# Mixing the tokens of the last units on VectorE instead of TensorE, with their scaling moved there and new call orders

## The reference

```python
# block 1: a long convolution per channel (K decays geometrically), a projection, layer norms
y = layer_norm(xn + gelu(conv(xn, K) + D_vec * xn) @ W_proj.T + b_proj, gamma, beta)
t = x + layernorm(y)
# block 2: tn = layernorm(t), tn_prev = tn of the token before (0 for the first of a sequence)
xr = mu_r * tn + (1.0 - mu_r) * tn_prev
xk = mu_k * tn + (1.0 - mu_k) * tn_prev
r = sigmoid(xr @ W_r.T)
k_act = square(relu(xk @ W_k.T))
out = t + layernorm(r * (k_act @ W_v.T))
```

## Time and profile before

| what | value |
|---|---|
| median of three runs | 150.51 us (150.22 to 150.79) |
| the profiled execution | 150.25 us, span 148.5 us, mean granted TensorE clock 0.988 |
| TensorE, busy | 135.5 us (91%) |
| VectorE, busy | 130.8 us (88%) |
| ScalarE, busy | 129.6 us (87%) |
| GpSimd, busy | 127.5 us (86%) |
| bytes moved | 8.99 MB |

### The profile page before, as it was taken

The page is one execution under the profiler, slowest core; times in us unless marked ns, Lnnn a source line. Parts: engine busy times, 40 slices in busy tenths (PEclk is TensorE's granted clock), DMA queues, the critical chain, the costliest instruction groups (busy, mean ns, idle before and its releaser), DMA issues.

```text
span 148.5 us, 3239 instructions
## 1 busy us (share of the span) xinstructions
PE 135.5 (91%) x950; PEld 116.0 (78%) x950; DVE 130.8 (88%) x372; ACT 129.6 (87%) x388; POOL 127.5 (86%) x176
## 2 busy tenths in 40 slices
PE   6778888989999999999999999999999999999910
PEld 6667787876988799797979797988887887777900
DVE  0989999999999988999997999998999899339981
ACT  4878999799699999979779999959998988999940
POOL 4599999998989988989896998978999899978282
PEclk9999999999999999999999999999999999999995
DMA  3999900000000002000200002200200200424524
GB/s 89 235 328 272 299 22 0 0 2 0 0 4 0 0 0 77 0 2 0 75 0 0 0 4 71 73 0 7 71 2 0 71 4 0 141 68 138 152 72 141
DMA packets 18705, 8.99 MB, mean 61 GB/s; under 512 B 1536, under 2 KB 18688, under 8 KB 18688
## 3 DMA queue, kind: packets, MB, share of 16 engines
q1 hardware_dynamic: 17840, 8.52, 19.7%
q10 hardware_dynamic: 848, 0.26, 0.7%
HBM read 4.59 MB, written 4.19 MB: 59 GB/s over the span
## 4 chain that ended last, share of the span: by engine, by line
PE 73%; POOL 17%; DVE 4%; DMA 2%; issue 1%; POOLq 1%; ACT 0%
PE ps_k L855 9%; PE ps_k L856 9%; PE ps_r L867 9%; PE ps_r L866 9%; PE ps_tv L876 9%; PE ps_z L833 7%; POOL x_r L227 5%; POOL xn_pow L236 5%; PE ps_tv L846 5%; PE ps_prefix L813 4%; PE ps_z L834 4%; PE ps_xT L805 3%; PE ps_prefix L819 2%; PE ps_prefix L815 2%; DMA a_col<-in_A_param 2%
## 5 line engine op out<-in xcount | busy, mean ns | idle before, releaser
L370 ACT ACTIVATE xn<-x_all,x_bias,x_r 128x128 f32<-128x128 f32 x64 | 26.4, 499 | 1.1 <-POOL x_bias L218 0.6
L867 PE MATMUL ps_r<-mixed_T,tsT 128*128 128x128 f32 x128 | 24.7, 275 | 0.0
L866 PE MATMUL ps_r<-mixed_T,tsT 128*128 128x128 f32 x128 | 24.7, 275 | 0.0
L833 PE MATMUL ps_z<-pv_T,gelu 128*128 128x128 f32 x128 | 22.1, 275 | 0.0
L426 ACT ACTIVATE f_normal<-f,out_bias,yf_r 128x128 f32<-128x128 f32 x48 | 19.8, 493 | 1.5 <-POOL out_bias L285 1.5
L236 POOL TENSOR_TENSOR xn_pow<-xn,pow_token 128x512 f32<-128x512 f32 x16 | 20.3, 1273 | 0.0
L866 PEld LDWEIGHTS ps_r<-mixed_T,tsT 128*128 128x128 f32 x128 | 19.5, 192 | 0.5 <-issue 0.5
L833 PEld LDWEIGHTS ps_z<-pv_T,gelu 128*128 128x128 f32 x128 | 19.4, 191 | 0.5 <-issue 0.5
L389 ACT ACTIVATE junk<-ps_z 128x128 f32<-128x128 f32 x64 | 16.7, 280 | 3.2 <-PE ps_z L834 3.2
L867 PEld LDWEIGHTS ps_r<-mixed_T,tsT 128*128 128x128 f32 x128 | 19.4, 192 | 0.0
L834 PE MATMUL ps_z<-ident,xnT 128*128 128x128 f32 x64 | 17.4, 273 | 0.0
(11 more groups left out here) (112 smaller groups left out, 360.1 us busy)
## 6 DMA issues: line engine op xcount, KB each, us to landing
out_x<-x_all SPq DMA_DIRECT2D x15, 256.0 KB, 2.2
x_all<-in_x SPq DMA_DIRECT2D x7, 512.0 KB, 6.0
x_all<-in_x SPq DMA_DIRECT2D x2, 128.0 KB, 2.8
x_all<-in_x SPq DMA_DIRECT2D x1, 256.0 KB, 3.2
out_x<-x_all SPq DMA_DIRECT2D x1, 128.0 KB, 1.8
out_x<-x_all ACTq DMA_DIRECT2D x1, 128.0 KB, 1.9
w_pv<-in_W_proj ACTq DMA_DIRECT2D x1, 64.0 KB, 2.6
w_pv<-in_W_v ACTq DMA_DIRECT2D x1, 64.0 KB, 4.5
```

The costliest lines, as they stand in the source:

```text
L370: last = a_.activation(tile(xn[u % D], j), xa(u, j), ACT.Identity, bias=col(x_bias, u, j), scale=col(x_r, u, j))
L833: t_.matmul(tile(ps_z[u % 3], j), tile(gelu[u % D], j), pv_T[:, 0, :], start=True, stop=False)
L866: t_.matmul(tile(ps_r, j), tsT[u % D][:, q, l + 1:l + 1 + P], mixed_T[:, 0, :], start=True, stop=False)
L867: last = t_.matmul(tile(ps_r, j), tsT[u % D][:, q, l:l + P], mixed_T[:, 1, :], start=False, stop=True)
```

## The change

For units 13, 14 and 15 the t is now centred and scaled by VectorE (`scale_t_vector`: four instructions per unit, which subtract the mean and multiply by the root), and no longer by GpSimd (13) or ScalarE (14, 15). For these units' gates, and for the keys of 14 and 15, the tokens are mixed before the product: `mix_difference` forms token minus predecessor from `tsT`, `mix_gates` and `mix_keys` multiply it by mu and add the predecessor, each one instruction over 512 columns. `gates` then makes 4 products in place of 8 and `keys` 1 in place of 2, with the plain weights `w_rk_T`. The mixed tokens lie in ring buffers that the first block has left (`xn`, `xn_pow`, `conv_scaled`). The lists of calls of GpSimd, ScalarE, VectorE and TensorE are written anew from beginning to end; SyncE's is as it was.

```diff
-T_ON_POOL = (1, 3, 5, 7, 9, 10, 11, 13)
+T_ON_POOL = (1, 3, 5, 7, 9, 10, 11)
+T_ON_VECTOR = (13, 14, 15)
+MIX_GATES = (13, 14, 15)
+MIX_KEYS = (14, 15)
...
+            def scale_t_vector(u):
+                dve.wait_ge(t_scale, u + 1)
+                after(dve, tT_ready, u - D + 1)
+                for j in range(TILES):
+                    last = v_.scalar_tensor_tensor(tile(t_scaled[u % D], j), xa(u, j), t_raw[:, u * TILES + j, 1:2],
+                                                   col(t_r, u, j).to_broadcast([P, P]), ALU.subtract, ALU.mult)
+                last.then_inc(ts_vector_ready, 1)
...
+            def mix_difference(u):
...
+                dve.wait_ge(tT_copied, u + 1)
+                v_.tensor_tensor(by_halves(xn[u % D]), tsT[u % D][:, :, 1:SEQ + 1], tsT[u % D][:, :, 0:SEQ],
+                                 ALU.subtract).then_inc(mix_differences, 1)
...
+            def mix_gates(u):
+
+                dve.wait_ge(mix_differences, mixed_units.index(u) + 1)
+                v_.scalar_tensor_tensor(by_halves(xn_pow[u % D]), by_halves(xn[u % D]), mu_cols[:, 0:1],
+                                        tsT[u % D][:, :, 0:SEQ], ALU.mult, ALU.add).then_inc(gate_mixed, 1)
+
+            def mix_keys(u):
+
+                dve.wait_ge(mix_differences, mixed_units.index(u) + 1)
+                v_.scalar_tensor_tensor(by_halves(conv_scaled[u % D]), by_halves(xn[u % D]), mu_cols[:, 1:2],
+                                        tsT[u % D][:, :, 0:SEQ], ALU.mult, ALU.add).then_inc(key_mixed, 1)
...
             def keys(u):
...
+                if u in MIX_KEYS:
+                    pe.wait_ge(key_mixed, MIX_KEYS.index(u) + 1)
+                    t_.matmul(ps_k[:], w_rk_T[:, 1, :], conv_scaled[u % D][:], start=True, stop=True).then_inc(k_ready, 1)
+                    return
...
             def gates(u):
...
+                if u in MIX_GATES:
+                    pe.wait_ge(gate_mixed, MIX_GATES.index(u) + 1)
+                    for j in range(TILES):
+                        last = t_.matmul(tile(ps_r, j), tile(xn_pow[u % D], j), w_rk_T[:, 0, :], start=True, stop=True)
+                    last.then_inc(r_ready, 1)
+                    return
```

More of the change, by code:

```diff
@@ L329, in _ @@
[L329 to L349, removed]
+            x_scale_tiles(0, 0, 2); x_scale_tiles(1, 2, 4); x_scale_of(1, 1, 1); xn_times_pow(0); x_scale_of(2, 2, 2)
@@ L840, in transpose_t @@
                     pe.wait_ge(ts_pool_ready, T_ON_POOL.index(u) + 1)
+                elif u in T_ON_VECTOR:
+                    pe.wait_ge(ts_vector_ready, T_ON_VECTOR.index(u) + 1)
                 else:
-                    pe.wait_ge(ts_ready, u + 1 - sum(v < u for v in T_ON_POOL))
+                    pe.wait_ge(ts_ready, u + 1 - sum(v < u for v in T_ON_POOL + T_ON_VECTOR))
                 after(pe, tT_copied, u)
@@ L891, in _ @@
-            prefix_sum(13); keys(6); project(11); values(5); transpose_xn(13); gates(6); transpose_t(7)
-            prefix_sum(14); keys(7); transpose_xn(14); project(12); values(6); gates(7); prefix_sum(15)
-            transpose_t(8); project(13); keys(8); values(7); gates(8); transpose_xn(15); transpose_t(9); project(14)
-            values(8); keys(9); transpose_t(10); gates(9); project(15); values(9); keys(10); transpose_t(11)
+            centre_bias(); keep_busy(3); transpose_xn(0); keep_busy(6); prefix_sum(0); keep_busy(6); transpose_pv()
@@ new lines, in _ @@
+            transpose_xn(1); prefix_sum(1); project(0); transpose_xn(2); prefix_sum(2); project(1); transpose_xn(3)
+            transpose_rk(); prefix_sum(3); project(2); transpose_xn(4); mix_weights(); prefix_sum(4); project(3)
+            prefix_sum(5); transpose_xn(5); project(4); transpose_t(0); prefix_sum(6); transpose_xn(6); gates(0)
+            keys(0); transpose_t(1); prefix_sum(7); keys(1); transpose_xn(7); values(0); project(5); project(6)
+            transpose_xn(8); gates(1); transpose_t(2); prefix_sum(8); values(1); gates(2); keys(2); transpose_t(3)
@@ new lines, in _ @@
+            prefix_sum(9); transpose_xn(9); project(7); values(2); keys(3); prefix_sum(10); gates(3); transpose_xn(10)
+            transpose_t(4); project(8); values(3); keys(4); transpose_xn(11); project(9); prefix_sum(11)
+            transpose_t(5); project(10); gates(4); prefix_sum(12); values(4); transpose_xn(12); gates(5); keys(5)
+            transpose_xn(13); prefix_sum(13); transpose_t(6); project(11); project(12); values(5); keys(6)
+            transpose_t(7); prefix_sum(14); transpose_xn(14); gates(6); keys(7); values(6); gates(7); transpose_xn(15)
@@ L895, in _ @@
+            transpose_t(8); project(13); values(7); keys(8); transpose_t(9); project(14); prefix_sum(15); gates(8)
+            values(8); keys(9); gates(9); transpose_t(10); project(15); values(9); keys(10); transpose_t(11)
             gates(10); values(10); keys(11); transpose_t(12); gates(11); values(11); keys(12); transpose_t(13)
             gates(12); values(12); keys(13); transpose_t(14); gates(13); values(13); keys(14); transpose_t(15)
-            gates(14); keys(15); values(14); gates(15); values(15)
+            gates(14); values(14); keys(15); gates(15); values(15)
```

134 lines of the change are left out of this document (76 added, 58 removed).

## The result

The changed kernel takes 153.48 us (median of five runs, 153.05 to 153.70), the kernel before 150.44 us beside it. The ratio is 1.0193 (95% interval 1.0176 to 1.0211), so it is 1.9% slower. The forecast was 152.2 us, 1.2% slower, with a range that holds the time. The profiled execution took 153.16 us, with a span of 151.4.

What follows compares the result with a forecast made beforehand. VectorE was to become the bound in the last units: 146.84 + 1.3 + 1.03 - 1.7 = 147.5 us for its end, then 3.0 of stores and 1.75 around the span, 152.2 us; range 148.3 to 155.0.

Steps and rivals of the forecast that it cites:

- What bounds: Last units: TensorE paces the end before the change; after it VectorE becomes the bound and limits what TensorE's saving is worth.
- TensorE's cut of 4.4 us: Last units: three gates with half the products save 2.7 us, two keys with one product for two 1.7 us.
- VectorE's added work of 7.9 us: Last units: twelve scaling instructions add 3.1 us and eight mixing instructions over 512 columns 4.8 us.
- Instructions held up, +1.03: VectorE beside GpSimd's additions: one more SBUF-only instruction loses 1.03 us; bounds -1.03 and +6.2.
- The third rival: GpSimd's additions hold up VectorE's new scalings and mixes, four stretches more than now: 155.3 us, chance 0.13.
- New orders ahead of 112.1, -1.7: VectorE before 112.1 us: the new call orders win half of its 3.47 us idle time, -1.7 us.
- ScalarE's and GpSimd's relief, set at nothing: Last units: scalings taken off both engines only bring a tanh or root earlier, for which VectorE won't wait; 0 us.
- Idle time that stays, +1.3: VectorE after 112.1 us: a fifth of its 6.56 us idle time stays, 1.3 us; bounds 0.4 and 3.3.
- The end: VectorE ends at 147.5 us, the last stores take 3.0 us more, and 1.75 us lie around the span.
- The signs: Expected profile: VectorE idle under 2 us after 112, busy 138 to 140; TensorE about 4 us less busy, with late gaps.
- The upper ends: Worst bounds of the terms for idle time, held-up instructions, new orders; all together given as 160 us.
- The first rival: VectorE keeps up: orders win 2.6 us before 112.1, no subtraction is held up, 0.9 us waits stay; 148.9 us, chance 0.30.

Runs made afterwards that it cites:

- the clock kept: Changed kernel plus 28 unread identity transposes on TensorE in its wait before the keys of unit 14: 152.39 us, ratio 1.0129 to the kernel before.
- the end rearranged: Changed kernel without the eight mixing calls, and VectorE's fused addition of unit 13 moved ahead of gate_half(0): 150.02 us, ratio 0.9972 to the kernel before.
- both at once: Changed kernel with GpSimd's additions of units 7 to 9 held back until unit 14's mix, plus 28 TensorE filler transposes: 152.66 us, ratio 1.0138 to the kernel before.

## Why the prediction was right, and by how much it was off

- **What bounds.** Right. TensorE's saving was worth only what VectorE could follow. Without the mixing TensorE paces the end again (the run without it). With all of it the chain that ended last goes through VectorE from 120.7 to 134.6 us and from 143.65 on; between the two it goes through TensorE, which runs at the half clock for the first half of that time.
- **TensorE's cut of 4.4 us.** The products are gone (28 instructions fewer), but I expected a busy time 4 us lower, and it is 0.6 lower, 3.8 short of the 4.4. Some 2.7 us of that went to the half clock: the four groups below take 2.05, 1.06, 1.92 and 1.59 us, against 1.10, 0.63, 1.06 and 1.13 with the clock kept. Of the other 1.1 us, 0.9 lies in the first 20 us (16.60 us against 15.68, for 104 instructions in both kernels), far ahead of the units that the change is about; what makes it I can't say. So the size of the cut was right to some 0.2 us.

```profile
134.58 2.05 PE L899 MATMUL ps_k<-conv_scaled,w_rk_T 128*128 128x512 f32 x2 [3.43 <-DVE conv_scaled L686]
136.42 1.06 PE L888 MATMUL ps_tv<-ident,t_scaled 128*128 128x128 f32 x4
137.27 1.92 PE L913 MATMUL ps_r<-w_rk_T,xn_pow 128*128 128x128 f32 x8
138.98 1.59 PE L928 MATMUL ps_tv<-pv_T,k_act 128*128 128x128 f32 x8
```

- **VectorE's added work of 7.9 us.** Nearly right. Two of the scalings take 1.14 and 1.13 us for four; the difference takes a step of 0.60 us where nothing waits for its result, a mix 0.67.
- **Instructions held up, +1.03.** This is the term that failed. It was +3.3: two of the scaling, one difference, one key mix, while the one subtraction that was long before (1303 ns) is long still (1310; it stands ahead of the gate of unit 12 now, not behind the mixing as the end of unit 13 otherwise does, and beside the addition of unit 5). My reason was that one addition only in the last 20 us had cost anything. But only one had met an instruction that it could hold up; before the change VectorE had hardly any there. The third rival's four stretches came, with 3.3 us in all for its 4.1 (the forecast's 1.03 and 3.1 more), and the run with the additions held back shows the cause.
- **New orders ahead of 112.1, -1.7.** They gave -2.56: VectorE worked 91.16 us from 20 to 112.1 where it worked 88.60. In the run with the new orders and the old scaling VectorE came as far ahead (91.19 us), and it was worth nothing there.
- **ScalarE's and GpSimd's relief, set at nothing.** Right for the changed kernel, where VectorE doesn't wait for a tanh any more. Without mixing no run sets it apart: from 1.0044 with their scaling to 0.9990 without are 0.8 us, but the orders behind the gate of unit 10 differ between these two as well.
- **Idle time that stays, +1.3.** 1.88 us (36.60 less 34.72). More than half is the wait of 1.0 us for the copy of unit 15, which comes late at the half clock; with the clock kept it is gone.
- **The end.** VectorE ends at 148.64 us, forecast 147.5; the span ends 2.8 us later, forecast 3.0; the execution is 1.76 us longer than the span, forecast 1.75.
- **The signs.** VectorE's little idle time after 112 us (1.9) and its share of the chain (12%) came as expected. Its busy time of 141.3 us is above the 138 to 140. The gaps of TensorE that are put down to VectorE stand in front of the keys and the transpose of unit 14 (3.4 and 0.7 us); those in front of the keys and the transpose of unit 15 didn't come.

By these figures 26.84 + 7.9 + 3.3 - 2.56 + 1.88 = 37.4 us after 112.1, against 36.6 in the trace; 0.8 us less work remains that I can't assign. The forecast was 1.3 us too low. Its largest term by far was the stretches, 2.3 too small; the orders, 0.9 better than set, made up for part of that, and that was luck: nothing but "half" stood behind their 1.7. That 153.48 lies nearer to the forecast than to the third rival's 155.3 is owed to it. The upper ends of the prediction add up to 161.1 us (146.84 + 3.3 + 6.2 + 4.75), not to 160. The first rival got its 2.6 us from the orders and lost all the same, since it needed that nothing was held up.

On the stretches the Trainium skill was nearer than my rows. "SBUF — State Buffer", section "Who interferes with whom", states that a VectorE instruction with two SBUF inputs contends with a GpSimd instruction that reads SBUF. The trace agrees for three forms of it: 1367 ns against 341, 1081 against 693, 1631 against 750. The same section says that `tensor_scalar` can contend with a single SBUF input, in its two-port modes; the rows agree there too, L638 with 1310 ns and L696 with 1319. It says as well that a single SBUF input outside those modes does not contend: the statistics at 131.02, with an addition beside them, took their usual 0.75 us.

## What to carry to other kernels

Work moved to a second engine to relieve the first is paid for by the second's idle time, and only where that idle time lies: two mixing instructions in a wait of 1.5 us cost nothing, eight of them placed by the units' order cost 2%. Before a VectorE instruction with two SBUF operands is placed, look for GpSimd instructions over large SBUF tiles beside it, and count the overlap as lost time on one of the two engines, or on both. Holding the GpSimd work back moved the loss to what stood there instead; the statistics lost nothing beside an addition, and so they would be the neighbours to try. And look at the gaps that a slower supplier leaves in front of TensorE, since what follows them may run at half the clock. When a run gains more than the last instruction of the path has moved, see what of it lies in the stores and outside the span before it is put down to the edit.

## What the runs showed of the hardware that was not expected

The fall of the clock was not foreseen: after an idle stretch of 3.4 us the granted clock was 0.50 for at least 4.6 us of steady work. Filling the stretch gained 1.0 us of time and 1.7 us of span in the median.

The time of an execution outside its span is not the same for all these kernels. It is 1.70 to 1.78 us in the runs of the changed kernel and 1.68 to 1.91 in those of before on the chip of the first experiments, but 2.38 to 2.97 without mixing and 2.23 to 2.40 with the clock kept. So without mixing the span is 0.65 us shorter than that of before (147.95 against 148.6, medians) while the time is the same. With the gates of unit 15 mixed it is 1.85 to 1.93 in four runs and 2.44 and 2.46 in two.

The traces show one thing that goes with it. In four of the twelve traced executions (without mixing, the clock kept, the end rearranged, both at once) one transfer of 16 KB on an instruction queue (q8) starts 1.75 to 1.78 us after the end of the span and takes 0.9 to 1.3 us; these four have 2.38 to 2.76 us outside the span. The other eight have no transfer there, and 1.73 to 1.90 us. So the longer tail goes with a load of instructions behind the last work. Why some executions have it and others not, no run shows. About 0.5 us of the distance between the rearranged end without and with the gates of unit 15 mixed lies there, not in the span.
